# Layer 3's expert loop finishes its rows and scatters them into the output

## The reference, cut to what matters

```
x = x + tanh(g_xattn[3]) * attention3(layernorm(x), ctx)
h = layernorm(x)
p = softmax(h @ Wr)                 # 8 experts
e = argmax(p);  p_max = max(p)      # one expert per token
y = gelu(h @ W1[e] + b1[e]) @ W2[e] + b2[e]
x = x + tanh(g_ffn[3]) * p_max * y  # the output
```

## Time and profile before

| | us |
|---|---|
| median of three runs | 713.46 (713.31 to 714.85) |
| the profiled execution's own time | 709.9 |
| its span, from first to last record | 708.2 |
| TensorE busy | 567.8 (80% of the span) |
| VectorE busy | 405.1 (57%) |
| GpSimd busy | 293.7 (41%) |

### The profile page before, as it was taken

One profiled execution on the slowest core, in us unless ns is written; L12 is line 12 of the kernel. 1 busy time (PEld: TensorE's weight loads), 2 busy tenths in 40 slices (PEclk: granted clock), 3 DMA queues, 4 the chain that ended last, 5 costly groups with the idle time before them and its releaser, 6 DMA issues.

```text
span 708.2 us, 13280 instructions
## 1 busy us (share of the span) xinstructions
PE 567.8 (80%) x3758; PEld 456.0 (64%) x3758; DVE 405.1 (57%) x1637; ACT 293.9 (41%) x732; POOL 293.7 (41%) x354
## 2 busy tenths in 40 slices
PE   5788779799848988239995899978899998954991
PEld 3466556699815666229993465754799846744991
DVE  3676655688757666402224876635488776653443
ACT  3455532244424564214441655532244335432660
POOL 3112567266610127634552110576166611272551
PEclk9999859999977897559997999759999997556996
DMA  8990012233181001112215000012123140012214
GB/s 270 225 420 5 24 34 62 75 87 86 57 292 65 2 8 40 37 50 61 68 55 155 13 1 2 31 42 80 44 85 91 52 119 1 0 45 76 64 48 127
DMA packets 56182, 54.84 MB, mean 77 GB/s; under 512 B 8200, under 2 KB 50976, under 8 KB 55056
## 3 DMA queue, kind: packets, MB, share of 16 engines
q1 hardware_dynamic: 48272, 39.75, 18.9%
q0 software_dynamic: 7840, 14.25, 6.2%
HBM read 34.99 MB, written 20.86 MB: 79 GB/s over the span
## 4 chain that ended last, share of the span: by engine, by line
PE 54%; DVE 12%; issue 10%; POOL 8%; ACT 5%; DVEq 5%; DMA 4%; SPq 0%; POOLq 0%; ACTq 0%
PE bank L861 17%; PE bank L873 11%; POOL slots L554 6%; PE bank L698 5%; PE bank L685 4%; DVE x L1530 3%; PE bank L849 2%; ACT pay L953 2%; DVE stat L1120 2%; PE bank L816 2%; PE bank L647 2%; PE bank L818 2%; PE bank L833 2%; DMA slots<-pay,pos 1%; PE bank L659 1%
## 5 line engine op out<-in xcount | busy, mean ns | idle before, releaser
L580 POOL DMA_INDIRECT result<-xn,row x133 | 131.6, 989 | 132.2 <-DVE row L1480 122.1
L554 POOL DMA_INDIRECT slots<-pay,pos x112 | 110.9, 990 | 57.4 <-issue 34.0
L517 POOL TENSOR_TENSOR rstd<-spread,minus_half 128x4 f32<-128x4 f32 (+1 forms) x33 | 34.2, 1036 | 207.2 <-DVE spread L1113 174.9
L861 PE MATMUL bank<-xnT,gat 128*128 128x128 f32 x808 | 111.1, 282 | 1.1 <-DVE gat L1489 1.1
L873 PE MATMUL bank<-w,hsh 128*128 (+1 forms) x752 | 106.1, 276 | 1.7 <-DVE hsh L1496 1.1
L861 PEld LDWEIGHTS bank<-xnT,gat 128*128 128x128 f32 x808 | 100.7, 196 | 2.5 <-ACT xnT L1046 1.3
L873 PEld LDWEIGHTS bank<-w,hsh 128*128 128x128 f32 x752 | 94.6, 192 | 2.4 <-issue 2.4
L698 PEld LDWEIGHTS bank<-vblk,probT 128*128 128x128 f32 x384 | 52.5, 207 | 37.3 <-ACT probT L993 25.9
L698 PE MATMUL bank<-vblk,probT 128*128 128x36 f32 x384 | 54.3, 290 | 14.1 <-ACT probT L993 11.1
L1046 ACT COPY xnT<-bank 128x128 f32<-128x128 f32 x133 | 35.6, 269 | 64.8 <-PE bank L849 59.8
L1507 DVE COPY xn<-bank 128x128 f32<-128x128 f32 x110 | 31.4, 285 | 50.4 <-PE bank L873 50.4
(11 more groups left out here) (233 smaller groups left out, 1042.1 us busy)
## 6 DMA issues: line engine op xcount, KB each, us to landing
xg<-slots SPq DMA_DIRECT2D x133, 64.5 KB
w<-in_w SPq DMA_DIRECT2D x4, 2048.0 KB, 11.8
pay<-result SPq DMA_DIRECT2D x21, 256.0 KB, 4.2
w<-in_w SPq DMA_DIRECT2D x1, 2560.0 KB, 19.0
w<-in_w SPq DMA_DIRECT2D x1, 2304.0 KB, 14.1
result<-xn,row POOLq DMA_INDIRECT x133, 2.2
slots<-zeros SPq DMA_DIRECT2D x1, 2064.0 KB, 25.8
slots<-pay,pos POOLq DMA_INDIRECT x112, 2.3
```

The costliest lines, as they stand in the source:

```text
L517: own(pool.tensor_tensor(rstd[:, lo:hi], spread[:, lo:hi], minus_half[:, lo:hi], ALU.pow))
L554: pool.indirect_dma_start(out=(slots1 if l == 1 else slots)[:, :], out_offset=bass.IndirectOffsetOnAxis(ap=pos[:, t, k:k + 1], axis=0), in ...
L580: pool.indirect_dma_start(out=result[:, :], out_offset=bass.IndirectOffsetOnAxis(ap=row[:, s % TURN:s % TURN + 1], axis=0), in_=ysb[:, s % ...
L861: last = pe.matmul(bank[2 + p][:, c * P:(c + 1) * P], weights[:, c * P:(c + 1) * P], xgT[:, p, :], start=True, stop=True)
```

## The change

Only layer 3 is changed. Its slots get 258 numbers instead of 129: the scaled token, the id, the finished weight (tanh of the gate over the sum of the exponentials) and the token's x after attention. They go to a table of their own, `slots3`; `pay` is read as one array `pay3` of 16 rows of 258. The weight must now be there before a group is scattered: `pick` makes the differences group by group, ACT takes their exponentials group by group, and a new `weights3` runs ahead of `place_rows`. In the expert loop `copy_y` gets a second DVE instruction, y * weight + x, and the scatter goes straight to the output. The load back, `combine` and the stores of layer 3 go. The loaded tiles lie in a ring of eight in the space of layer 1's first weights (`w1[1]`, named w_1 in the rows of order), and a buffer is free once `copy_y` is done.

```diff
+        pay3 = pay[:].rearrange("p k t c -> p (k t c)").rearrange("p (t c) -> p t c", c=2 * ROW)
+        x3 = pay3[:, :, ROW + 1:2 * ROW]
+        xg3 = w1[1][:].rearrange("p e n -> p (e n)")[:, 0:TURN * 2 * ROW].rearrange("p (q c) -> p q c", c=2 * ROW)
-        zeros = sb("zeros", [P, ROW])
+        zeros = sb("zeros", [P, 2 * ROW])
+        slots3 = nc.dram_tensor("slots3", [E * REGION, 2 * ROW], F32, kind="Internal").ap()
...
+        def loaded(l, k):
+            if l == 3:
+                return filled3[k % TURN], 16 * (k // TURN + 1)
+            return filled[k % RING], 16 * (k // RING + 1) + ring_base(l, k % RING)
+
+        def rows_of(l, k):
+            return xg3[:, k % TURN] if l == 3 else xg[:, k % RING]
...
-                        sp.dma_start(slots[bass.ds(r, P), :], zeros[:]).then_inc(padded, 16)
+                        sp.dma_start(src[bass.ds(r, P), :], zeros[:, 0:src.shape[1]]).then_inc(padded, 16)
...
-                    if s >= RING:
+                    if l == 3 and s >= TURN:
+                        sp.wait_ge(Z["t_ysb"], s + (base - TURN + 1))
+                    elif l < 3 and s >= RING:
...
+                if l == 3:
+                    return
                 for k in range(TOPK[l]):
                     sp.dma_start(pay[:, k, 0:GT // 2, 0:D],
...
-            for g in range(NG):
-                sp.wait_ge(Z["x_done"], g + 1)
-                sp.dma_start(out_d[g * S:(g + 1) * S, :].rearrange("(t p) d -> p t d", p=P),
-                             x[:, g * GT:(g + 1) * GT]).then_inc(out_done, 16)
-            sp.wait_ge(out_done, 16 * NG)
...
+                if l == 3:
+
+                    pool.wait_ge(scat[2], 16 * 2 * NTILE)
+                    own(pool.iota(pay3[:, :, P], [[P, NTILE]], base=0, channel_multiplier=1,
...
-                        out=result[:, :], out_offset=bass.IndirectOffsetOnAxis(ap=row[:, s % TURN:s % TURN + 1], axis=0),
+                        out=(out_d if l == 3 else result)[:, :], out_offset=bass.IndirectOffsetOnAxis(ap=row[:, s % TURN:s % TURN + 1], axis=0),
...
-                exp_logits(l)
+                if l == 2:
+                    exp_logits(l)
+                    return
+                act.wait_ge(Z["r_top"], 3 + g + 1)
+                act.activation(ex[:, g * GT:(g + 1) * GT], ex[:, g * GT:(g + 1) * GT], ACT.Exp).then_inc(Z["r_ex"], 1)
...
+                if l == 3:
+                    ts = slice(g * GT, (g + 1) * GT)
+                    dve.tensor_tensor(ex[:, ts], top[:, ts], top[:, ts, 0:1].to_broadcast([P, GT, 8]),
+                                      ALU.subtract).then_inc(Z["r_top"], 1)
...
+            def weights3(g):
+
+                ts = slice(g * GT, (g + 1) * GT)
+                dve.wait_ge(Z["r_ex"], 3 + g + 1)
+                dve.tensor_reduce(sums[:, ts], ex[:, ts], AX.X, ALU.add)
+                dve.drain()
+                dve.reciprocal(over[:, ts], sums[:, ts])
+                dve.drain()
+                dve.tensor_scalar(pay3[:, ts, ROW], over[:, ts], tg[:, 7:8], None, ALU.mult)
...
-                        dve.tensor_tensor(ysb[:, q, :], bank[6 + p][:, 0:D], b2[:, bass.ds(e * D, D)], ALU.add).then_inc(Z["t_ysb"], 1)
+                        dve.tensor_tensor(ysb[:, q, :], bank[6 + p][:, 0:D], b2[:, bass.ds(e * D, D)], ALU.add)
+                        dve.drain()
+                        src = rows_of(l, k)
+                        dve.scalar_tensor_tensor(ysb[:, q, :], ysb[:, q, :], src[:, ROW:ROW + 1], src[:, ROW + 1:2 * ROW],
+                                                 ALU.mult, ALU.add).then_inc(Z["t_ysb"], 1)
...
-            for g in range(NG):
-                combine(LAYERS - 1, g)
```

More of the change, by code:

```diff
@@ L252, in flamingo @@
         back_half = sem("back_half")
-        out_done = sem("out_done")
+        filled3 = [sem(f"filled3_{q}") for q in range(TURN)]
         def grown(per_layer, l):
@@ L387, in _ @@
             sp.dma_start(slots1.rearrange("(t p) d -> p t d", p=P),
-                         zeros[:].unsqueeze(1).to_broadcast([P, SEG * CAP // P, ROW])).then_inc(zero_done, 16)
+                         zeros[:, 0:ROW].unsqueeze(1).to_broadcast([P, SEG * CAP // P, ROW])).then_inc(zero_done, 16)
             for h in range(HEADS):
@@ L395, in _ @@
             for l in range(LAYERS):
-                src = slots1 if l == 1 else slots
+                src = (slots, slots1, slots, slots3)[l]
                 if l != 1:
@@ L554, in scatter @@
                         pool.indirect_dma_start(
-                            out=(slots1 if l == 1 else slots)[:, :],
+                            out=(slots, slots1, slots, slots3)[l][:, :],
                             out_offset=bass.IndirectOffsetOnAxis(ap=pos[:, t, k:k + 1], axis=0),
-                            in_=pay[:, k, t, :], in_offset=None,
+                            in_=pay3[:, t, :] if l == 3 else pay[:, k, t, :], in_offset=None,
                             bounds_check=(SEG * CAP if l == 1 else E * REGION) - 1, oob_is_err=False).then_inc(scat[l], 16)
@@ L745, in transpose_routed @@
                 for t in range(GT):
-                    last = pe.transpose(bank[1][:, t * P:(t + 1) * P], pay[:, 0, g * GT + t, 0:D], ident[:])
+                    last = pe.transpose(bank[1][:, t * P:(t + 1) * P], (pay3 if l == 3 else pay[:, 0])[:, g * GT + t, 0:D], ident[:])
                 last.then_inc(Z["r_xt"], 1)
@@ L1087, in _ @@
                     (at["tokens_r"], GROUPS, copy_routed),
-                    (at["pick"] + PERIOD[l] * (NG - 1), (0,) if l == 2 else (), exp_of_picked)], shared)
+                    (at["pick"] + PERIOD[l] * (NG - 1), (0,) if l == 2 else (), exp_of_picked),
+                    (at["pick"], three, exp_of_picked)], shared)
+                if l == 1:
+                    exp_logits(l)
                 if l in (1, 3):
-                    exp_logits(l)
                     preload(ACT.Gelu_apprx_tanh if l == 1 else ACT.Gelu)
@@ L1114, in before_root, with statistics @@
                 last.then_inc(done, 1)
-            def statistics(g, lo, done, twice=False):
+            def statistics(g, lo, done, twice=False, x=x):
                 dve.drain()
@@ L1280, in into_x3 @@
                 dve.wait_ge(Z["a_pr"], n_at(3, g) + 1)
-                xs = x[:, g * GT:(g + 1) * GT].rearrange("p t d -> p (t d)")
-                dve.scalar_tensor_tensor(xs, bank[6][:], tg[:, 3:4], xs, ALU.mult, ALU.add).then_inc(Z["a_x"], 1)
+                ts = slice(g * GT, (g + 1) * GT)
+                dve.scalar_tensor_tensor(x3[:, ts], bank[6][:].rearrange("p (t d) -> p t d", t=GT), tg[:, 3:4], x[:, ts],
+                                         ALU.mult, ALU.add).then_inc(Z["a_x"], 1)
             def pick(l, g):
@@ L1306, in pick @@
                                   ALU.is_equal).then_inc(Z["r_pick"], 1)
-                if g == NG - 1:
+                if l < 3 and g == NG - 1:
                     dve.tensor_tensor(ex[:], top[:], top[:, :, 0:1].to_broadcast([P, NTILE, 8]),
                                       ALU.subtract).then_inc(Z["r_top"], 1)
+            def weights3(g):
+                ts = slice(g * GT, (g + 1) * GT)
+                dve.wait_ge(Z["r_ex"], 3 + g + 1)
[4 more added lines that the diff above has]
+                dve.tensor_scalar(pay3[:, ts, ROW], over[:, ts], tg[:, 7:8], None, ALU.mult)
             def place_rows(l, g):
+                if l == 3:
+                    weights3(g)
                 dve.wait_ge(Z["r_rank"], g_at(l, g) + 1)
@@ L1476, in ids @@
                 def ids(k):
-                    q, i = k % RING, k % TURN
-                    dve.wait_ge(filled[q], 16 * (k // RING + 1) + ring_base(l, q))
-                    dve.scalar_tensor_tensor(row[:, i:i + 1], xg[:, q, D:D + 1], valid[:, k:k + 1],
+                    i = k % TURN
+                    dve.wait_ge(*loaded(l, k))
+                    dve.scalar_tensor_tensor(row[:, i:i + 1], rows_of(l, k)[:, D:D + 1], valid[:, k:k + 1],
                                              away[:, k:k + 1], ALU.mult, ALU.add).then_inc(Z["t_id"], 1)
@@ L1519, in experts @@
                 steps(n, step, (mybir.EngineType.DVE, l) if l != 1 else None)
-                weights(l)
+                if l < 3:
+                    weights(l)
             def combine(l, g):
@@ L1529, in combine @@
                         for t in range(t0, t1):
-                            last = dve.scalar_tensor_tensor(x[:, t, :], pay[:, k, t, 0:D], wts[:, t, k:k + 1], x[:, t, :],
+                            dve.scalar_tensor_tensor(x[:, t, :], pay[:, k, t, 0:D], wts[:, t, k:k + 1], x[:, t, :],
                                                             ALU.mult, ALU.add)
@@ L1536, in combine @@
                     dve.drain()
-                if l == LAYERS - 1:
-                    last.then_inc(Z["x_done"], 1)
             def combine_last(l, g):
```

17 lines of the change are left out of this document (8 added, 9 removed).

## The result

| | before | after |
|---|---|---|
| median of the timed runs, us | 713.46 | 710.82 |
| the profiled execution's own time, us | 709.9 | 709.62 |
| its span, us | 708.2 | 707.9 |
| predicted | | 704.1 (702.4 to 707.8) |

The change gives 0.38%: the ratio to the kernel before is 0.9962 (0.9944 to 0.9981), some 2.7 us of the 9.4 that I forecast. The sign is right, the size is not, and the time lies outside the range.

The account below looks back on a forecast made before the run. PE's pace bounds layer 3's loop (1.89 us a tile), POOL the routing, latencies the tail. Terms -10.35 + 0 + 0.14 + 0.5 + 0.2 + 0.14 = -9.4 us, from 713.46 to 704.1 us, range 702.4 to 707.8.

Parts of the forecast that it names:

- The tail: After layer 3's loop: load back, additions, stores and their wait go, 11.2 us; net about -10.35 us.
- the program's own end: After the last landing: 0.4 us of the 11.2 kept as an end that remains.
- The added instruction in the tail: On DVE before the last scatter: 0.35 us plus a gap of 0.08, delaying that scatter by 0.43 us.
- The bytes: Routing scatters, pads and first tile loads, rows doubled to 1032 bytes: +0.5 us congestion, +0.2 us load.
- Routing: Layer 3's routing: DVE's added subtraction delays the first scatter, the other added work is hidden; +0.14 us (0 to 0.74).
- a sign of being wrong: Routing: the prediction counts as wrong if POOL waits for DVE there; no size given.
- rival C: Routing: POOL makes descriptors in two pieces, a scatter takes up to 1.94 us, +15.5 us; 719.6 us, chance 0.03.
- Start: Constants at the kernel's start: `zeros` twice as wide lengthens POOL's first memset; +0.14 us (0 to 0.21).
- Loop: Layer 3's expert loop: the added 0.43 us per tile is hidden, with 0.24 us of cover left; cost 0.
- Rival B: Expert loop: the added instruction waits for the scatter before it, 2.20 us a tile against 1.89; 710.7 us, chance 0.10.
- Rival A: Routing and loop: congestion 2.0 us instead of 0.5, and the loop costs 2 us; 707.6 us, chance 0.10.
- What would show it: Signs in the later profile: span ends 0.3 to 0.5 us after the last landing, 1.89 us a tile, scatters 0.97.

Follow-up runs that it names:

- Experiment 1: Changed kernel without GpSimd's drain at the end of the block: 706.25 us, 0.9911 of the kernel before; once more 707.0 us, 0.9883.
- experiment 2: Kernel before, with only GpSimd's drain at the end of the block left out: 713.56 us, ratio 1.0003.
- experiment 6: Changed kernel, drain kept, only the tile loads cut to 129 numbers a row, scatters and pads still 258: 712.61 us, 0.9964 of the kernel before.
- experiment 7: Changed kernel without the end drain, plus 20 unused matmuls on TensorE before layer 3's first expert tile: 704.89 us, 0.9852; once more 703.33 us, 0.9877.
- 8: Kernel before, drain kept, plus 18 unused matmuls on TensorE before layer 3's first expert tile: 712.88 us, ratio 0.9967.
- experiments 5: Changed kernel, drain kept, layer 3's slots, pads and loads at 129 numbers a row: 708.35 us, 0.9901 of the kernel before.
- 3: Changed kernel, with GpSimd waiting for its last four scatters to land before the end drain: 713.53 us, 0.9974 of the kernel before.
- 4: Changed kernel without the end drain, with a GpSimd drain behind tile 8's scatter in layer 3's loop: that drain took 6.92 us; no timed median given.

## Why the prediction was wrong

**The tail: the step that failed.** "I keep 0.4 of the 11.2 as the program's own end." I bounded the end by what lies between the landing of the last store and the end of the span, and so took it for granted that nothing else was under way in those 11.2 us. GpSimd's drain was, for 7.6 us from the last scatter's start. What is left after SP has seen the landing is 707.9 - 702.5 = 5.4 us, and some 0.2 ahead of that, not 0.4 in all. Experiment 1 gives 5.0 us of it back and experiment 2 shows that before it cost nothing. This one term is 5.2 of the 6.7 us that I was off. The chain of waits of the kernel before held only 0.22 us of that drain (at 694.72), since the chain names only what ended last; the list of what each engine's queue did at the end of the block held all of it.

**The added instruction in the tail** was sized rightly: 699.00 - 698.63 = 0.37 to its start and 0.35 of its own, 0.72 from the bias add's start where the add alone took 0.29: 0.43.

**The bytes: right in kind, too small.** I had 0.5 for the congestion and 0.2 for the load. Landing +0.87 (+0.94 by the means of experiment 6), load +0.31, and then a thing that I had no term for: the loop starts at the low clock. Landing to last scatter grew by 1.55 us. With the clock full from the first tile in both kernels (7 and 8) the difference is 50.25 - 49.5 = 0.75, about what the load and the added instruction come to (0.31 + 0.43). The other 0.8 goes with TensorE's clock. Its timeline at the loop's first transpose, in the kernel before and then in the changed one, idle time at the end:

```profile
646.75 0.47 PE L849 MATMUL bank<-ident,xg 128*128 128x128 f32 x1 [6.94 <-DMA xg<-slots]
```

```profile
650.77 0.48 PE L860 MATMUL bank<-ident,w 128*128 128x128 f32 x1 [8.07 <-DMA w<-slots]
```

and windows of the two, columns as in the earlier trace rows:

```profile
650.00:652.00 2.00, 2.00 (x16) 2.00 (x16) 0.36 (x2) 1.70 (x8) 0.00 (x0) 0.79 0.13 33
652.00:654.00 2.00, 2.00 (x21) 2.00 (x20) 0.85 (x3) 1.33 (x7) 0.43 (x1) 1.00 0.01 4
```

```profile
650.00:656.00 6.00, 4.99 (x22) 4.70 (x23) 1.33 (x5) 2.10 (x9) 0.00 (x0) 0.50 0.60 163
```

Before, TensorE had been idle for 6.94 us, and the chain of waits has the first transpose at full speed (0.11) at 652.24, 5.5 us after the loop's first transpose. In the changed kernel it had been idle for 8.07 us, and that point comes at 657.10, 6.3 us after the first transpose. Once started, PE has no gap over 0.24 us in either up to there; the 4.99 of 6.00 in the last window is the wait for the first loads. With the clock full from the start it comes after 4.5 us (655.10 to 659.58 in experiment 7). The nine profiles without extra matmuls fall into two groups: idle for 6.42 to 7.24 us and then 5.49 to 5.61 us to full speed (the kernel before, with and without its drain, and experiments 5 and 6), or idle for 7.75 to 8.43 us and then 5.97 to 6.50 us (the changed kernel and experiments 1, 3 and 4). Whether the longer idle time does it or the wide loads behind it, these runs can't tell. The Trainium skill (TensorE: Matmul & The Clock Gate, section "What's actually happening") says that the low clock is the idle state and activity releases it; experiment 7 agrees, with 0.81 and then 1.00 under the extra matmuls.

**Routing: 0.25 for my 0.14.** The subtraction moves the root by 0.11: from the first reduction of the softmax ahead of it to the root's start it is 621.05 - 615.66 = 5.39 us, against 618.33 - 613.05 = 5.28. Another 0.14 comes behind the root: from its start to the first scatter 623.03 - 621.05 = 1.98 us, against 620.17 - 618.33 = 1.84. This one is a wait that I had ruled out:

```profile
621.99 0.22 DVE L1363 TENSOR_REDUCE pos<-place 128x8 uint32<-128x64 f32 x1
...
623.03 1.04 POOL L561 DMA_INDIRECT slots<-pay,pos  x1 [0.69 <-issue]
```

The scatter starts 0.82 us after `pos` is done at 622.21. It takes the same time at layer 2's first scatter, where the trace names `pos` as what POOL waited for (448.17 to 448.99). I had compared the end of `pos` with the end of POOL's root, and left out this way from DVE to POOL. So POOL did wait for DVE in the routing, which I had named as a sign of being wrong, but by 0.14 us only. The scatters of the wide rows took no longer on POOL (rival C is refuted):

```profile
L561 POOL DMA_INDIRECT slots<-pay,pos x16: 967/972/1036, 623.0 to 643.9; - x16
```

**Start.** PE's first matmul at 6.06 instead of 5.96: +0.10 for my 0.14.

**Loop.** 0 was right, with 0.30 us of cover left where I had 0.24. Rival B is refuted by the 1.90 us per tile, though its 710.7 is almost the time that was measured: that is coincidence.

**The sum again**, by what was measured: end -5.6, landing +0.87, landing to last scatter +1.55 (added instruction, load, clock), routing +0.25, start +0.10. That is -2.8 us; the timed runs say -2.7. That the two come so close is partly luck, since the landing alone varies by 0.86 us between profiles with wide rows, and the timed interval spans 2.6 us.

**Rival A** named the bytes and came near on them (+1.5), but put the other 2 us into the loop, where nothing was lost. None of my cases had an end that stayed, so the range was too narrow on the side that happened. "What would show it" did say that the span should end 0.3 to 0.5 us after the last landing, and that line fails first.

**A version that beats both** is the changed kernel without GpSimd's last drain and with the extra matmuls: 0.9852, and 0.9877 when run again. By their intervals alone it can't be told from the one without the matmuls (0.9911 and 0.9883); by the profiles it is 1.5 to 2.1 us shorter between landing and last scatter.

## What to carry to other kernels

When a change cuts off the end of a program, list what every engine's queue still does after the point where the new end will be, and take the latest of these as the new end; the chain that ended last shows only what is cut. Where GpSimd has issued indirect DMAs and another engine waits for their landing, leave its drain at the block's end out. Where a phase of latencies ahead of a TensorE loop grows, count the loop's start at the low clock too, or fill the gap with matmuls that nobody reads.

## What the runs showed of the hardware that I had not expected

- A drain of GpSimd behind indirect DMAs takes 6.44 us when they have landed, 7.64 from the start of the last one, and 6.92 in the middle of a loop. The Trainium skill (VectorE: DVE Perf Modes, section "The DRAIN you can't avoid") gives about 12 ns for the drains that the runtime puts ahead of and behind a kernel on all five engines. Those at the end of this kernel's block are the kernel's own (GpSimd's goes with the edit of experiment 1), and in the changed kernel they took from 7 ns (SP) to 7637 ns (GpSimd), so that figure does not cover them.
- Twelve microseconds of difference in where a stage starts: the last routing scatter lies between 641.00 and 652.66 in the twelve profiled executions, though the kernels differ little up to there, and 8.6 us apart in two executions of one kernel. It goes with TensorE's granted clock in the layers ahead. From 30 to 70 us that was 0.87 to 0.91 in three executions, whose first scatter of all came at 77.5 to 79.8, 0.83 in five (79.9 to 81.0) and 0.79 in four (81.2 to 82.5). From 376 to 440 us it was 0.92 in nine; in the three with 0.84 to 0.89 the way from layer 1's last routing scatter to layer 2's first took 141.2 to 143.6 us instead of 137.6 to 138.1. Why the clock differs between executions no run shows.
- Twenty matmuls whose result nobody reads took 1.5 to 2.1 us out of the stage behind them, by the profiles.
